# First stage of a graph kernel: tile bounds from whole rows and one split row, the unit table inside the loop, the bias add on GpSimd

## The reference, cut to what matters

```python
x = x + gnn0(layernorm(x), edge_index) + bias0   # attention over the edges of a node, 4 heads
x = x + ffn0(layernorm(x))                       # 6 experts, 2 of them per node
x = x + gnn1(layernorm(x), edge_attr, ...)       # attention with edge features, 1 head
x = x + ffn1(layernorm(x))                       # 8 experts, all of them
```

## Time and profile before

| | |
|---|---|
| median of 3 runs | 4462.22 us (4454.69 to 4463.83) |
| the profiled execution | 4459.09 us, of which its span is 4457.3 us |
| busy in the span | PE 3334.8 us (75%), DVE 2672.3 (60%), POOL 2067.7 (46%), ACT 1572.2 (35%) |
| mean granted clock of TensorE | 0.814 |

### The profile page before, as it was taken

The page is one execution under the profiler, slowest core; times in us unless marked ns, Lnnn a source line. Parts: engine busy times, 40 slices in busy tenths (PEclk is TensorE's granted clock), DMA queues, the critical chain, the costliest instruction groups (busy, mean ns, idle before and its releaser), DMA issues. The chain is left out here.

```text
span 4457.3 us, 72937 instructions
## 1 busy us (share of the span) xinstructions
PE 3334.8 (75%) x16240; PEld 2512.1 (56%) x16240; DVE 2672.3 (60%) x8449; ACT 1572.2 (35%) x4383; POOL 2067.7 (46%) x2095
## 2 busy tenths in 40 slices
PE   5276667776666789964566666666659999999999
PEld 3144444444444578843344444444438888888888
DVE  8488999999987866654565565656555322222221
ACT  2233343334332224431333333333323434333343
POOL 0477777777770034365777777777730000000000
PEclk9677787777876579966677777777779999999999
DMA  4344444444454147644444444444461000000000
GB/s 123 81 106 107 107 108 107 107 107 107 107 99 87 37 126 193 171 114 99 107 106 106 106 106 106 105 106 105 105 80 35 5 7 5 7 5 7 5 7 8
DMA packets 386919, 369.85 MB, mean 83 GB/s; under 512 B 253644, under 2 KB 313708, under 8 KB 386562
## 3 DMA queue, kind: packets, MB, share of 16 engines
q0 software_dynamic: 107072, 272.84, 24.9%
q1 hardware_dynamic: 277094, 92.40, 9.4%
q10 hardware_dynamic: 2396, 0.84, 0.1%
HBM read 324.13 MB, written 41.59 MB: 82 GB/s over the span
## 5 line engine op out<-in xcount | busy, mean ns | idle before, releaser
L694 POOL DMA_INDIRECT g_G<-rows,g_pack x1856 | 1806.8, 973 | 756.1 <-issue 480.0
L727 PE MATMUL bank<-g_G,g_MB 128*125 128x260 f32 x1856 | 654.7, 499 | 207.1 <-DVE acc L933 205.9
L933 DVE SCALAR_TENSOR_TENSOR acc<-acc,g_c,bank 125x65 f32 (+1 forms) x2320 | 618.2, 315 | 147.5 <-PE bank L727 73.1
L1375 DVE SCALAR_TENSOR_TENSOR X<-bank,e_cw,X 125x256 f32 (+1 forms) x400 | 175.2, 479 | 795.6 <-PE bank L1201 795.6
L727 PE MATMUL bank<-g_G,g_M 128*125 128x257 f32 x1856 | 633.6, 489 | 20.7 <-DVE acc L933 20.6
L727 PEld LDWEIGHTS bank<-g_G,g_MB 128*125 128x125 f32 x1856 | 418.4, 243 | 348.9 <-DVE acc L933 242.4
L1271 ACT ACTIVATE e_h<-bank,e_bi_c,e_sc_c 128x250 f32<-128x250 f32 x800 | 403.6, 555 | 560.3 <-PE bank L1192 422.3
L798 ACT ACTIVATE g_mt_d<-bank,unode 125x256 bf16<-125x256 f32 x928 | 383.3, 463 | 457.7 <-PE bank L712 457.2
L727 PEld LDWEIGHTS bank<-g_G,g_M 128*125 128x125 f32 x1856 | 418.3, 241 | 147.4 <-DVE acc L933 26.5
L1201 PE MATMUL bank<-e_w,e_h 128*125 128x256 f32 x1600 | 379.3, 380 | 3.1 <-ACT e_h L1271 3.1
L1192 PE MATMUL bank<-e_h,e_w 128*128 128x250 f32 x1600 | 377.6, 378 | 1.2 <-ACT e_h L1271 1.2
(11 more groups left out here) (299 smaller groups left out, 4141.3 us busy)
## 6 DMA issues: line engine op xcount, KB each, us to landing
g_G<-rows,g_pack POOLq DMA_INDIRECT x1856
acc<-in_edge_attr SPq DMA_DIRECT2D x50, 476.0 KB
g_pack<-edge_pack SPq DMA_DIRECT2D x928, 2.0 KB
g_drow<-edge_dst SPq DMA_DIRECT2D x928, 1.0 KB
expert_out<-x_y SPq DMA_DIRECT2D x54, 256.0 KB
g_qe<-edge_q SPq DMA_DIRECT2D x464, 1.0 KB
rows<-acc SPq DMA_DIRECT2D x25, 227.5 KB
rows<-n_T SPq DMA_DIRECT2D x25, 224.9 KB
```

The lines of the kernel that those rows point to most:

```text
L694: nc.gpsimd.indirect_dma_start(G[:, r, q, :], None, rows_d[l], bass.IndirectOffsetOnAxis(ap=pack[:, r, q, 0:1], axis=0)).then_inc(S(p + f" ...
L727: mm_ = nc.tensor.matmul(sum_bank(r, k, u)[0:TN, 0:HW], left, G[:, rk, q, :], start=(c == 0), stop=(c == C - 1))
L933: ins = nc.vector.scalar_tensor_tensor(at, at, c1[:, rk, u, h:h + 1], sum_bank(r, k, u)[0:TN, h * W:(h + 1) * W], ALU.mult, ALU.add)
L1375: ins = nc.vector.scalar_tensor_tensor(xt, bank[4 + u][0:TN, 0:D], cw[:, r, u, e:e + 1], xt, ALU.mult, ALU.add)
```

## The change

- **The counts.** A row of `dst` holds 850 sorted edges. DVE compares, for all tiles at once, each tile's bound with the last edge of each row (`whole`: the row lies below the bound as a whole) and with the first (`torn`: the one row that the bound splits). Whole rows count 850 each. PE picks each tile's split row by two products of `torn` with `dst`, 512 and 338 columns, and DVE counts in the 50 picked rows, one tile to a partition, in two instructions. Two small products give the bounds in all partitions. `dst` is shifted by 16384 for it. The 50 counts over all of `dst` go.
- **The unit table.** The same steps now stand in DVE's slots: the split rows' counts in slot 0, the eight steps on the bounds in slot 1, the table in slot 2. SP writes the table ahead of its loop and reads it back behind the loop, ahead of the last loads and stores.
- **The bias add** to X goes from DVE to POOL for this stage, in a loop of its own.

```diff
+    v.wait_ge(S("dst_in"), ND)
+    nc.vector.tensor_scalar(dstz[:, :], dst_t[:, :], float(-SHIFT), None, ALU.add).then_inc(S("dstz"), 1)
...
+    nc.vector.tensor_scalar(whole[:, :], bound[0:EP, :], dstz[:, EC - 1:EC], None, ALU.is_gt).then_inc(S("whole"), 1)
+    v.wait_ge(S("whole"), 1)
+    nc.vector.scalar_tensor_tensor(torn[:, :], bound[0:EP, :], dstz[:, 0:1], whole[:, :], ALU.is_gt, ALU.subtract).then_inc(S("torn"), 1)
+    nc.vector.tensor_scalar(whole_n[:, :], whole[:, :], float(EC), None, ALU.mult).then_inc(S("whole"), 1)
...
-    v.wait_ge(S("dst_in"), ND)
-    nc.vector.tensor_copy(dstf[:, :], dst_t[:, :]).then_inc(S("dstf"), 1)
...
-    v.wait_ge(S(p + "bias"), 16)
-    def count(t):
-        nc.vector.tensor_scalar(below[:, :], dstf[:, :], bound[0:EP, bass.ds(t, 1)], 0.0, ALU.is_lt, ALU.add,
-                                accum_out=cnt[:, bass.ds(t + 1, 1)]).then_inc(S("counted"), 1)
...
+    def torn_rows():
+        v.wait_ge(S("row_picked"), 1)
+        nc.vector.tensor_scalar(below[:, 0:512], bank[3][0:NT, :], col[0:NT, :], 0.0, ALU.is_lt, ALU.add, accum_out=part[:, 0:1])
+        step(nc.vector.tensor_scalar(below[:, 512:EC], bank[6][0:NT, 0:EC - 512], col[0:NT, :], 0.0, ALU.is_lt, ALU.add, accum_out=part[:, 1:2]))
+        step(nc.vector.tensor_tensor(part[:, 0:1], part[:, 0:1], part[:, 1:2], ALU.add))
+        v.wait_ge(S("fills"), 1)
+        v.wait_ge(S("whole"), 2)
+        nc.vector.tensor_scalar(part_d[:, :], ident[0:NT, 0:NT], part[:, 0:1], None, ALU.mult).then_inc(S("part_d"), 1)
...
-    if grouped(i, 1):
+    if l == 1 and grouped(i, 1):
         nc.vector.tensor_tensor(xt, xt, bias[:, :].unsqueeze(1).broadcast_to([TN, GT, D]), ALU.add)
-    if l == 0 and grouped(i, 0):
-        for u in range(GT):
-            count(i * GT + u)
+    if l == 0 and isinstance(i, int) and i == 0:
+        torn_rows()
+    if l == 0 and isinstance(i, int) and i == 1:
+        tile_units()
+    if l == 0 and isinstance(i, int) and i == 2:
+        unit_table()
...
 # GpSimd
+    pool.wait_ge(S(p + "bias"), 16)
+    def slot(i, r, t):
+        if grouped(i, 1):
+            pool.wait_ge(S(p + "xn"), i)
+            xt = X[:, bass.ds((i - 1) * GT, GT), :]
+            nc.gpsimd.tensor_tensor(xt, xt, bias[:, :].unsqueeze(1).broadcast_to([TN, GT, D]), ALU.add).then_inc(S(p + "shifted"), 1)
+    run(pool, slot)
...
 # TensorE, ahead of the weights' wait
+    pe.wait_ge(S("torn"), 1)
+    nc.tensor.matmul(bank[3][0:NT, :], torn[:, :], dstz[:, 0:512], start=True, stop=True)
+    nc.tensor.matmul(bank[6][0:NT, 0:EC - 512], torn[:, :], dstz[:, 512:EC], start=True, stop=True).then_inc(S("row_picked"), 1)
...
 # TensorE, slot 1
+    pe.wait_ge(S("part_d"), 1)
+    nc.tensor.matmul(bank[7][:, 0:NT], ones[0:EP, :], whole_n[:, :], start=True, stop=False)
+    nc.tensor.matmul(bank[7][:, 0:NT], ones[0:NT, :], part_d[:, :], start=False, stop=True).then_inc(S("ptr_mm"), 1)
...
 # SyncE
     for i in range(4):
         slot(i, i, 0)
+    sp.wait_ge(S("units_made"), 1)
+    sp.dma_start(unit_d.rearrange("(p k) t -> p k t", p=P), unit_t[:, :, :]).then_inc(S("unit_out"), 16)
+    sp.dma_start(ubase_d.rearrange("(p k) -> p k", p=P), ub[:, :]).then_inc(S("unit_out"), 16)
```

More of the change, by code:

```diff
@@ L44 @@
 KU = 4
+SHIFT = 16384
 AE = 64
@@ L188, in rows @@
                 pad_row = sb("pad_row", [1, HW], F32, sc)
-                below = sb("below", [EP, EC], F32, sc)
-                cnt = sb("cnt", [EP, NT + 1], F32, sc)
+                below = sb("below", [NT, EC], F32, sc)
+                int_col = sb("int_col", [P, 1], I32, sc)
+                col = sb("col", [P, 1], F32, sc)
+                whole = sb("whole", [EP, NT], F32, sc)
+                whole_n = sb("whole_n", [EP, NT], F32, sc)
+                torn = sb("torn", [EP, NT], F32, sc)
+                part = sb("part", [NT, 2], F32, sc)
+                part_d = sb("part_d", [NT, NT], F32, sc)
                 int_n = sb("int_n", [P, P], I32, sc)
@@ L285, in _ @@
                         sp.dma_start(unit_i[:, :], unit_d.rearrange("(o u) t -> o u t", o=1)[:, :, 0], allow_slow_non_contiguous=True).then_inc(S("unit_in"), 16)
+                        for i in range(NG - 5, NG + 2):
+                            slot(i, i % 4, i // 4)
                         sp.wait_ge(S("pad_out"), 80)
@@ L439, in _ @@
                         nc.vector.tensor_copy(wext[:, :, D + 1:D + 2], attr[:, :, :]).then_inc(S(p + "wext"), 1)
-                    v.wait_ge(S(p + "bias"), 16)
-                    def count(t):
[L444 to L448, removed]
-                        nc.vector.tensor_scalar(below[:, :], dstf[:, :], bound[0:EP, bass.ds(t, 1)], 0.0, ALU.is_lt, ALU.add,
-                                                accum_out=cnt[:, bass.ds(t + 1, 1)]).then_inc(S("counted"), 1)
+                    if l == 1:
+                        v.wait_ge(S(p + "bias"), 16)
@@ new lines, in tile_units @@
+                    def tile_units():
+                        v.wait_ge(S("ptr_mm"), 1)
+                        step(nc.vector.tensor_copy(ptr[:, 1:NT + 1], bank[7][:, 0:NT]))
+                        step(nc.vector.tensor_tensor(width[:, :], ptr[:, 1:NT + 1], ptr[:, 0:NT], ALU.subtract))
+                        step(nc.vector.tensor_scalar(width_i[:, :], width[:, :], float(UE - 1), None, ALU.add))
+                        step(nc.vector.tensor_scalar(nunit_i[:, :], width_i[:, :], LOG_UE, None, ALU.arith_shift_right))
+                        step(nc.vector.tensor_copy(nunit[:, :], nunit_i[:, :]))
+                        step(nc.vector.tensor_tensor_scan(ends[:, :], nunit[:, :], zeros[:, :], 0.0, ALU.add, ALU.add))
+                        step(nc.vector.tensor_tensor(starts[:, :], ends[:, :], nunit[:, :], ALU.subtract))
+                        step(nc.vector.scalar_tensor_tensor(off[:, :], starts[:, :], -float(UE), ptr[:, 0:NT], ALU.mult, ALU.add))
@@ L511, in _ @@
                     if l == 0:
[L512 to L532, removed]
@@ L533, in _ @@
-                        step(nc.vector.tensor_tensor(hot[:, :, :], jf[:, :].unsqueeze(2).broadcast_to([P, KU, NT]),
-                                                     tile_f[:, :].unsqueeze(1).broadcast_to([P, KU, NT]), ALU.is_equal))
-                        step(nc.vector.tensor_tensor(hot[:, :, :], hot[:, :, :], off[:, :].unsqueeze(1).broadcast_to([P, KU, NT]), ALU.mult))
-                        step(nc.vector.tensor_reduce(sf[:, :], hot[:, :, :], AX.X, ALU.add))
-                        step(nc.vector.scalar_tensor_tensor(sf2[:, :], uf[:, :], float(UE), sf[:, :], ALU.mult, ALU.add))
```

50 lines of the change are left out of this document (29 added, 21 removed).

## The result

The changed kernel takes 4439.75 us (median of 5 runs, 4428.14 to 4440.16) against 4463.83 us (5 runs, 4454.69 to 4476.84) for the kernel before, run beside it: a ratio of 0.9937, 95% interval 0.9916 to 0.9957. The profiled execution takes 4428.14 us, its span is 4426.4 us, the mean granted clock 0.818. The span is 30.9 us shorter than before's, and the stage accounts for it: the next stage begins at 121.25 us in place of 151.93, 30.7 earlier. What follows it lasts 4305.2 us, before 4305.4.

What follows compares the result with a forecast made beforehand. VectorE was taken to bound the first stage; head 3.4, loop 17.6 and tail 11.5 us sum to 32.5 off the profiled 4459.09, giving 4426.6, and 4428 as median, range 4419 to 4445.

Steps and rivals of the forecast that it cites:

- the sum: Whole first stage: head 3.4, loop 17.6 and tail 11.5 us, together 32.5 off the profiled 4459.09, giving 4426.6.
- The loop: Groups 3 to 24: 21 slots of 3.65 us plus 1.65 for one low-clock slot, 78.3 against 95.87, gain 17.6.
- the two undisturbed turns of the earlier trace: Loop before: two spans between ScalarE first copies that waited for nothing on VectorE, 3.60 and 3.68 us; 3.65 taken.
- The rival of a low slot in every third: Loop: TensorE's clock still falls in every third slot, loop gain only 7.7 us, 4436.5 in total; chance 0.17.
- The tail: Behind the last group: table and round trip gone, next stage at 140.4 instead of 151.93 on the old clock, gain 11.5 us.
- The head: Before the loop: 0.86 ahead of slot 0, slot 0 +0.2, slot 1 -0.5, slot 3 +2.89; gain 3.4 us.
- the prediction's own sign: Head: the forecast counts as wrong if slots 1 to 3 last longer than 14.3 us together.
- those of slots 2 and 3: Head: 1.60 us to the statistics' end plus table (2.91) or packing (3.13): 4.51, nothing gained, and 4.73, gain 2.89.
- The rival of the blocked engines: Head: GpSimd's adds meet the table's first comparison and the packing's copies, costing 2.2 to 4.6 us; chance 0.14.
- Slot 1: Head: 1.60 us, then about 1.5 waiting for the bounds' product, then eight steps of 1.95; 5.0 in all, loss 0.5.
- The add on GpSimd: First stage: 1.1 us an add, bounds 0.69 and 2.3; hidden, only the closing barrier waits for it, costing nothing.
- the ring: Loop, TensorE and ScalarE: products, four copies out of PSUM, copy of next transposes, next products; 3.65 us a slot.

Runs made afterwards that it cites:

- c_after: The changed kernel unaltered, run again beside the kernel before: 4429.46 us, ratio 0.9915 to 0.9943; next stage at 121.80 us.
- c_after_2: The changed kernel unaltered, run once more beside the kernel before: 4433.71 us, ratio 0.9921 to 0.9948; next stage at 119.73 us.
- e3: The kernel before with only the bias add moved to GpSimd, counts kept on VectorE: 4444.55 us, ratio 0.9946 to 0.9973; next stage at 138.05 us.
- e10: The changed kernel with GpSimd's adds of groups 1 and 2 done at the stage's end: 4432.91 us, ratio to before 0.9910 to 0.9937.
- e2: The changed kernel with the unit table and its transfers back behind the loop: 4437.11 us, ratio to before 0.9932 to 0.9959; next stage at 126.54 us.
- after: The changed kernel in its first comparison with the kernel before: 4439.75 us, ratio 0.9916 to 0.9957; next stage at 121.25 us.
- e8: The changed kernel with transposes ahead of products, two adds last, packing transfers and table reads behind the last X load: 4413.82 us, ratio to before 0.9874 to 0.9903.
- e1: The changed kernel with the bias add back on VectorE: 4432.55 us, ratio to before 0.9922 to 0.9949; next stage at 122.89 us.
- e4: The changed kernel with each slot's transposes ahead of the products, ScalarE's order turned likewise: 4426.79 us, ratio to before 0.9897 to 0.9927.

## Why the prediction was right, point by point

4428 us (4419 to 4445) was forecast as the median, with faster at 0.93; it was 4439.75, and the profiled execution took 4428.14 where the sum gave 4426.6. The profiled execution was the fastest of five, and the other four took 4438.66 to 4440.16; the forecast had put the median only 1.4 us above the profiled one. What was slower in those four no profile shows. The medians of c_after and c_after_2, 4429.46 and 4433.71, lie nearer to 4428. So the stage is what the sum got right, within 1.8 us of 32.5, and that by errors that partly cancel: the head gave 1.6 us less than forecast and the tail 0.7 less, the loop 0.5 more.

- **What bounds the stage, right.** VectorE set the pace and no longer does. e3 shows it from the other side: 0.69 us less a slot on VectorE was worth 12.2 us of the loop while VectorE set the pace.
- **The loop, right in size.** 78.3 us forecast for 21 groups, 77.77 measured, so 18.1 us gained where 17.6 was forecast. The slots are 3.60 and 3.69, as the two undisturbed turns of the earlier trace rows had said.
- **The clock, right.** It stays up (0.98 in the loop) but for one slot at its start, where a group's products take 3.68 us; c_after has two such slots around that place, c_after_2 one ahead of it, e10 none. The rival of a low slot in every third fell. What it took to keep the clock up isn't isolated: in e3, with slots of 3.88 and the counts still there, it was at 0.94.
- **The tail, nearly.** 11.5 forecast, 10.8 measured. e2 splits it: 8.0 the table, 2.7 the bounds. From the last transposes to the last copy's end it is 4.55 us where 4.26 was taken over from before, and store and barrier took 4.34 where 3.88 was summed; the 0.3 us for the store's signal in that sum stands in no row.
- **The head, wrong by half.** 3.4 forecast, 1.8 measured. By the prediction's own sign this part was wrong: slots 1 to 3 lasted 16.23 us together (16.79 to 33.02), and 14.3 was the limit. The terms that failed are those of slots 2 and 3, "is 4.51" and "is 4.73", which took VectorE's operations at their old lengths: measured 4.87 and 5.69, and 4.31 and 4.62 in e10. The rival of the blocked engines, given 0.14 and 2.2 us, happened on top of the forecast instead of in its place: it cost 1.63 us (e10), below its price since neither meeting cost a whole add. In slot 2 the add met the minimum, not the table's first comparison, which began just ahead of it. Slot 1 was short too, forecast 5.0 and measured 5.67, in e10 as well as after: VectorE waited 1.99 us for the bounds' product (20.38), where 1.5 was estimated. Slot 0 gave 0.4 us of that back.
- **The add on GpSimd.** 1.1 us taken, 1.27 measured, both inside the bounds. "Nobody waits for it" holds in the loop, where it starts with the normalisation's end and VectorE has nothing that it holds for long. It doesn't hold in the head, nor in the tail, where the comparison that makes `fresh` took 1.75 us beside an add (112.04), and 0.69 in e2 and e8 without one. There it was hidden.
- **What wasn't asked.** Each part was priced by itself against the kernel before. By that the add's move would be worth 21 times 0.69, or 14.5 us, and e3's loop gains 12.2; but with the counts gone e1's slots are no longer than after's. The sum as a whole was right since it took the ring as the loop's price and didn't add up what VectorE lost.

## What to carry to other kernels

When work leaves the engine that sets the pace, price the loop by the next ring, read from those turns in the trace that waited for nothing else, and not by the work removed; a second edit on the same engine may then be worth nothing. Work that is moved to GpSimd isn't free for VectorE even where nobody waits for it: look which VectorE operations start inside it, and put it beside those that it doesn't lengthen (below). When a loop gets faster, look next at the queue that feeds it: here a burst of transfers that had been harmless stood ahead of the last load, and VectorE waited 9.5 us for it.

## What the runs showed of the hardware that was not expected

- An add of two inputs on GpSimd lengthens some VectorE operations that start inside it: a minimum of 4 columns from 0.17 to 0.72 us, a cast of 850 columns from 0.60 to 1.67, two normalisations of 256 columns from 0.72 to 1.18, a comparison of 511 columns with two inputs from 0.69 to 1.75. Each lost what was left of the add when it started, less 0.13 to 0.24 us by the profile's spans. GpSimd's own add grew from 1.27 to 1.58 beside the packing. Others that ran inside an add kept their lengths: a reduction of 200 columns its 0.36 us (after, 24.35), the statistics their 0.75 and the reciprocal its 0.17 (e8). The Trainium skill, "SBUF — State Buffer", section "Who interferes with whom", names casts, `tensor_scalar` and operations with two inputs as those that can wait for GpSimd, and leaves out the form of `tensor_scalar` that also writes its sum. The lengthened operations here are all of the first kinds; on the form with the sum no run here decides, as the counts of e3 start 0.2 us ahead of an add or in its last 0.1 to 0.2 us.
- That add, 125 x 512 in fp32, takes 1.27 us by itself, 1.8 times VectorE's 0.69. The Trainium skill, "GPSIMD Engine Reference", section "Engine selection", says about twice; the runs agree.
- A load was late by its place among SyncE's issues: X, asked for at 90.04 in e4, reached VectorE at 96.64 after a wait of 9.50 us; asked for at 79.48 in e8, ahead of the burst, it kept nobody waiting. The DMA engines' share from 75 to 95 us doesn't tell the two apart: 0.83 in e4 and 0.87 in e8.
